# Graph network on one core: who adds the edge gates, how often TensorE signals, and how long the ring of gathered rows is

## The reference

```python
ea = silu(edge_attr @ We + be)                  # one row of 128 per edge: the "gates"
for l in range(4):                              # block 1: the four "layers"
    msg = relu(x[src] + ea)
    agg = segment_sum(msg, dst, num_segments=n)
    h = silu((x + agg) @ W1[l] + b1[l]) @ W2[l] + b2[l]
    x = layernorm(x + h) * gamma[l] + beta[l]
# blocks 2 and 3: three "convs" (two with degree norms, one plain with a self weight)
out = segment_sum(h[src], col, num_segments=n)
```

## Time and profile before

| | |
|---|---|
| median of three executions | 10520.3 us (10517.32 to 10532.23) |
| the profiled execution | 10607.1 us, of which the span from first to last instruction is 10605.0 us |
| busy in the span | PE 54%, PEld 37%, DVE 29%, ACT 9%, POOL 59% |
| TensorE clock granted | 0.716 of full speed on average |

### The profile page before, as it was taken

One profiled execution on the slowest core, in us unless ns is written; L12 is line 12 of the kernel. 1 busy time (PEld: TensorE's weight loads), 2 busy tenths in 40 slices (PEclk: granted clock), 3 DMA queues, 4 the chain that ended last, 5 costly groups with the idle time before them and its releaser, 6 DMA issues.

```text
span 10605.0 us, 107124 instructions
## 1 busy us (share of the span) xinstructions
PE 5675.4 (54%) x23750; PEld 3922.0 (37%) x23751; DVE 3028.2 (29%) x7366; ACT 949.0 (9%) x1767; POOL 6216.3 (59%) x6738
## 2 busy tenths in 40 slices
PE   3566637566775667656675666653334333333334
PEld 2333437333443334433343333333333333333234
DVE  3444577212221122312222122331122112231222
ACT  1111100111111111101111111110000000000000
POOL 3655536565555655466554655546666666656665
PEclk7566659777887788878788778875566556665666
DMA  5777755332323323233332323221111111111111
GB/s 167 218 219 218 203 139 155 90 88 82 85 75 86 87 82 85 79 85 87 83 83 75 88 81 81 77 59 45 47 49 48 46 46 49 48 46 46 47 49 47
DMA packets 796948, 945.08 MB, mean 89 GB/s; under 512 B 269045, under 2 KB 530448, under 8 KB 796302
## 3 DMA queue, kind: packets, MB, share of 16 engines
q0 software_dynamic: 213408, 463.35, 16.4%
q1 hardware_dynamic: 474970, 390.60, 13.2%
q10 hardware_dynamic: 108436, 89.99, 2.6%
HBM read 797.55 MB, written 152.25 MB: 90 GB/s over the span
## 4 chain that ended last, share of the span: by engine, by line
another core or an unknown queue 44%; PE 18%; issue 13%; DVE 9%; DVEq 3%; POOL 0%; SPq 0%; ACT 0%; DMA 0%; ACTq 0%; POOLq 0%
PE ps_big L1119 8%; PE ps_seg L1126 5%; DVE onehots L1715 2%; DVE sums L1746 2%; DVEq L453 1%; PE ps_seg L1197 1%; PE ps_big L1197 1%; PE ps_big L1063 1%; PE ps_t L1038 1%; DVE gate L1894 1%; DVE h_res L1898 0%; DVE group_stats L1783 0%; PE ps_seg L1063 0%; PE ps_big L987 0%
## 5 line engine op out<-in xcount | busy, mean ns | idle before, releaser
L871 POOL DMA_INDIRECT rows<-node_rows,idx_all x5488 | 5209.8, 949 | 3470.5 <-SPq L713 1590.0
L1119 PE MATMUL ps_big<-rows,ident 128*128 (+1 forms) x1960 | 1221.8, 709 | 1386.0 <-DVE onehots L1715 1249.5
L1746 DVE TENSOR_TENSOR sums<-sums,ps_seg 128x128 f32 x1342 | 385.5, 287 | 5141.3 <-remote 3368.8
L1126 PEld LDWEIGHTS ps_seg<-onehots 128*128 128x128 f32 x7840 | 1206.0, 223 | 899.0 <-issue 735.5
L1126 PE MATMUL ps_seg<-onehots 128*128 128x128 f32 x7840 | 1236.4, 309 | 260.6 <-issue 168.0
L1715 DVE SCALAR_TENSOR_TENSOR onehots<-ps_mm,away 128x512 f32<-128x512 f32 x1975 | 1349.3, 684 | 21.4 <-issue 13.8
L1197 PE MATMUL ps_seg<-rows,onehots 128*128 (+1 forms) x2952 | 613.8, 372 | 1235.4 <-DVE onehots L1715 595.8
L1119 PE MATMUL ps_big<-q_res,ident 128*128 (+1 forms) x1960 | 1153.9, 674 | 150.9 <-issue 123.0
L1119 PEld LDWEIGHTS ps_big<-rows,ident 128*128 128x128 f32 x1960 | 412.0, 224 | 2036.2 <-DVE onehots L1715 1461.7
L871 POOL DMA_INDIRECT sums<-kv_rows,idx_all x784 | 743.4, 948 | 548.2 <-SPq L711 281.2
L1197 PEld LDWEIGHTS ps_seg<-rows,onehots 128*128 128x128 f32 x2952 | 536.7, 272 | 1301.7 <-DVE onehots L1715 619.0
(11 more groups left out here) (215 smaller groups left out, 2974.4 us busy)
## 6 DMA issues: line engine op xcount, KB each, us to landing
q_res<-gates_by_edge SPq DMA_DIRECT2D x784, 256.0 KB
rows<-node_rows,idx_all POOLq DMA_INDIRECT x5488
rows<-dst_padded SPq DMA_DIRECT2D x196, 256.0 KB
value_rows_by_edge<-sums SPq DMA_DIRECT2D x196, 256.0 KB
gates_by_edge<-gate ACTq DMA_DIRECT2D x196, 256.0 KB
rows<-value_rows_by_edge SPq DMA_DIRECT2D x196, 256.0 KB, 3.5
node_rows<-h_res ACTq DMA_DIRECT2D x49, 448.0 KB
sums<-kv_rows,idx_all POOLq DMA_INDIRECT x784
```

The source lines that it names most:

```text
L871: pool.indirect_dma_start(target[:, r, j, :], None, table, bass.IndirectOffsetOnAxis(ap=idx_all[:, c * J + j:c * J + j + 1], axis=0), elem ...
L1119: last = nc.tensor.matmul(ps_big[u][:, :], ident[:, :], chunk_words(source, slot, 0, CHUNK), start=n == 0, stop=n == 1)
L1126: last = nc.tensor.matmul(ps_seg[u][:, 0:D], onehots[:, u, j, :], msg[:, u, j, 0:D], start=j == 0, stop=j == J - 1)
L1746: V.tensor_tensor(mine, mine, seg_four[(n - 1) % depth][:, 0:D], ALU.add).then_inc(agg_added, 1)
```

## The change

In the layers the gates are no longer added by TensorE. ScalarE copies a step's gates from SBUF to a PSUM bank, VectorE adds the rows to it into one of eight message buffers, ScalarE takes the relu in place, and TensorE does the product alone. In layers and convs TensorE raises `segsum_ready` once per four steps, at the end of a turn; four products lie side by side in one PSUM bank, and two banks take turns. VectorE waits once per turn, adds four products, and makes the four 0/1 matrices for the turn two ahead (eight sets instead of two or four). Slots of the ring are freed in the layers by VectorE's `rows_added`; in the convs by `segsum_ready` of the turn, and the ring of the convs has 14 slots instead of 7. The parts of a group stand one turn later in the code. The words that steer the turns are laid out anew by 25 small DMAs (14 ahead of the layers, 11 ahead of the convs).

```diff
-                def relu(u, added):
-                    act.wait_ge(gates_added, added)
-                    nc.scalar.activation(msg[:, u, :, 0:D], ps_big[u][:, :].rearrange("p (j d) -> p j d", d=D), ACT.Relu)\
-                        .then_inc(msg_ready, 1)
+                def copy_gates(slot, landed):
+                    act.wait_ge(rows_ready, landed)
+                    nc.scalar.copy(ps_gates[:, :], q_flat[:, ds(slot, CHUNK)]).then_inc(gates_copied, 1)
+
+                def relu(n, half, added):
+                    act.wait_ge(rows_added, added)
+                    nc.scalar.activation(msgs[:, half, n, :], msgs[:, half, n, :], ACT.Relu).then_inc(msg_ready, 1)
...
+                def add_rows(i, slots, half):
+                    for n in range(UNROLL):
+                        dve.wait_ge(gates_copied, dve.compute_val(i * UNROLL + add_base + (n + 1)))
+                        V.tensor_tensor(msgs[:, half, n, :], ps_gates[:, :],
+                                        rows[:, ds(up_to(slots[n], (RING - 1) * SLOT), CHUNK)], ALU.add).then_inc(rows_added, 1)
+
+                def add_sums(i, windows, half, ahead=True):
+                    upto = [dve.compute_val(i * UNROLL + base + (n + 1)) for n in range(UNROLL)]
+                    dve.wait_ge(segsum_ready, dve.compute_val(i + turn_base + 1))
+                    for n in range(UNROLL):
+                        mine = sums[:, ds(up_to(windows[n], (WINDOWS - 1) * AGGW), D)]
+                        dve.wait_ge(agg_added, upto[n])
+                        V.tensor_tensor(mine, mine, ps_seg[half][:, n * D:n * D + D], ALU.add).then_inc(agg_added, 1)
+                    for n in range(UNROLL if ahead else 0):
+                        mark_step(i * (UNROLL * J) + (n + 2 * UNROLL) * J, n, (onehots, marks_late)[half])
+
+                def steps_of(i, words, half, more=True):
+                    add_rows(i, words[0:UNROLL], half)
+                    if len(words) > UNROLL:
+                        add_sums(i - 1, words[UNROLL:2 * UNROLL], 1 - half, more)
...
+                    for j in range(J):
+                        last = nc.tensor.matmul(ps_seg[half][:, n * D:n * D + D], marks[:, n, j, :],
+                                                msgs[:, half, n, j * D:j * D + D], start=j == 0, stop=j == J - 1)
+                    if n == UNROLL - 1:
+                        last.then_inc(segsum_ready, 1)
...
-                chunk_pass(k, "edges", gates_added, l * N_STEP, also=lambda: layer_loads(l))
+                chunk_pass(k, "edges", rows_added, l * LAST, also=lambda: layer_loads(l))
...
+                for r in range(WIDE):
+                    sp.sem_inc(slot_free, 1)
+
+                def free_turn(turn):
+                    freed, regs = load_free(turn * RING - WIDE, RING)
+                    for r in range(RING):
+                        sp.wait_ge(segsum_ready, ((freed[r] + (UNROLL - 1)) >> (UNROLL.bit_length() - 1)) + begun)\
+                            .then_inc(slot_free, 1)
```

424 lines of the change are left out of this document (292 added, 132 removed).

## The result

The changed kernel takes 10898.7 us (median of four, 10876.3 to 10912.4) where the kernel before takes 10518.8: a ratio of 1.0365, 95% interval 1.0347 to 1.0383. It is **slower by 380 us**; 260 us less were forecast. The profiled execution is the shortest of the four, 10876.3 us, with a span of 10874.5.

The account below looks back on a forecast made before the run. POOL's gathers (980 us a pass) were the floor, with slot waits added by a loop of held TensorE signals. Layers -110 and convs -150 gave -260 us, 10520 to 10260; range 9,700 to 10,560.

Parts of the forecast that it names:

- The signal is held by time: Layers and convs: matmul signals are held while POOL gathers, from some 5 us after restart, until POOL pauses.
- Convs, -150 us: Convs: three turns a round cut slot waits from 155 to 90 us; -50 a pass, three times.
- Bounds: 0: Convs: the bound with no gain, two turns and 32 us a round, as before the change.
- Layers, a step's work: Layers: copy 0.585, addition 0.685, relu 0.597 us in strict sequence, 2.2 us a step with handovers, hidden behind POOL.
- Layers, 2.7 turns a round and 9.5 us of pause: Layers: slot waits of 215 us make a pass 1254 us against 1285.4; -28 us, four times, -110.
- The bound of 1359: Layers: the slow bound of a pass in us, at two turns a round and pauses of 10.5 us.
- Code: Rival, 0.04: VectorE's longer layer loop stops 4.56 us for instruction fetch in 30 rounds; 550 us over four layers, 10,800.
- VectorE's wait costs more than the loop did: Rival, 0.17: two turns a round and 11 us pauses in layers, +90 us a layer, -50 a conv; 10,730.
- The pass' end: Layers: 57 us between passes, 47.3 and 10 more for slower last steps and a last signal covering four.
- The 25 small DMAs: Ahead of layers and convs: issued while SP waits for the last store, costing nothing; uncovered, 25 x 0.4 = 10 us.
- Rare signals aren't held: Rival, 0.20: one signal per turn goes free; layers 1060, convs 1030 us a pass; whole 9,230, halfway 9,900.
- Slots are late for another reason: Rival, 0.05: if SyncE itself is slow, slot waits stay and only ends of passes move; 10,520.

Follow-up runs that it names:

- after_again: The changed kernel, unchanged, run again for its trace on one chip with the kernel before, where signals are late: 10908.5 us, ratio 1.0381.
- short_loop: The changed kernel with the last layer's residual code taken out of VectorE's loop for the first three layers (body 227 instructions, not 355): 10882.7 us, ratio 1.0357.
- pad_before: The kernel before with 200 never-reached small instructions added in VectorE's loop over a layer's turns: 10803.4 us, ratio 1.0282.
- two_banks_again: The changed kernel with ScalarE copying gates to two PSUM banks in turn, one step ahead of its relu, on a late-signal chip: 11131.7 us, ratio 1.0573.

## Why the prediction was wrong, step by step

**The signal is held by time (wrong; this is the step that failed).** I wrote that a matmul's signal is held while POOL gathers, "from some 5 us after its restart, and is let go when POOL pauses". The lateness was read rightly, its law was not. A signal also came out in the middle of a run, in the earlier trace rows already. What the runs support is that the instructions ahead of the signal count: with half of them a layer takes 51 to 75 us less, with twice as many, and twice the work, the kernel 1,135 us more, and four times the signals cost nothing that shows. The error in the convs follows from it, and in the layers it left me without the right question, which was what else stands in line.

**Convs, -150 us (measured +15 to +46).** I took three turns a round, 61/3 x 4.44 = 90 us of slot waits. A round is two turns and a little more, 128 to 143 instructions in the median; the pauses are 5.0 us: 61/2 x 5.0 = 152, measured 147.8, where it was 155.4. The ring of 14 and VectorE's greater lead were spent on a place that was not the limit. "Bounds: 0" was the case that came, and the pass' end added 6.5 and 19.6 us in the gaps, where I had allowed 15.

**Layers, a step's work (right).** ScalarE's copy takes 0.582 us, VectorE's addition 0.691, the relu 0.629; a step 1.98 us where I had 2.2 (groups of instructions by form of the changed kernel, as in the earlier trace rows):

```profile
L1896 DVE TENSOR_TENSOR score<-ps_big,stock 128x512 f32<-128x512 f32 x976 | 674.8, 691 | 2200.6 <-issue 1395.8 <-ACT ps_big L1524 804.7
...
L1528 ACT ACTIVATE score<-score 128x512 f32<-128x512 f32 x976 | 614.3, 629 | 3225.7 <-DVE score L1896 2647.8 <-issue 577.9
...
L1524 ACT COPY ps_big<-stock 128x512 f32 x976 | 568.0, 582 | 629.9 <-issue 590.6 <-POOLq L952 39.3
```

**Layers, 2.7 turns a round and 9.5 us of pause (the second step that failed: a term was missing).** In the second layer 23 pauses exceed 6 us, 61/23 = 2.65 turns each. That it fits so well is luck: the line of 6 us was drawn afterwards, and in after_again it gives 20 pauses, 3.05 turns. They last 10.6 us on average, 245 us where I had 215; the missing 1.1 us is less than the 4.9 of the branch, which falls into every other one. And there are 27 shorter ones, 82 us together, for which the sum had no term: a slot is freed by an addition, an addition every 2 us comes after each late signal, and POOL waits for the next piece each time. Pass: 982 + 327 + 58.5, less what counts twice = 1353.8, for 1254 forecast. Of the 100 us that are missing 30 are the pause's price and some 70 the short ones. The bound of 1359 holds it, but by another sum. What else moved in the layers: TensorE's granted clock in the second one fell from 0.80 to 0.61 in the mean, and a product that runs in one piece takes 1.16 to 2.08 us where most took 1.05. Its share no run separates.

**Code (given 0.04; its trigger and stop came, its price did not).** The loop's body grew and each round stopped at the branch, with the packets to show it, 4.88 us for 4.56. But not 550 us: by short_loop's layers 45 to 55, an estimate, of the 253 to 299 us that the layers lost. I had given it 0.04 because the earlier trace rows show hardly any fetch now; but the kernel before has a body of 163 instructions, and its row says nothing of one of 355. The counterpart, pad_before, which stops in each of 61 turns, cost 2.8% on its own.

**VectorE's wait costs more than the loop did (given 0.17).** Its +90 a layer is near to what came (+63 to +75), and VectorE's work behind the late signal is what lies in the pauses. Of all the cases it comes nearest. But its two turns a round hold in two_banks_again, and here there were 2.65 to 3.05.

**The pass' end (right in the layers).** 58.5 us, forecast 57. **The 25 small DMAs (right):** SyncE issues the 14 ahead of the layers from 1892.46 to 1901.92 and the 11 ahead of the convs from 7330.86 to 7338.79, 0.7 us each for the 0.4 that I took, and then still waits until 1923.09 and 7365.06 for the last store. The gap ahead of the first conv grew by 21.5 us (76.65 for 55.13) all the same, ahead of the first of ScalarE's last two stores. **Rare signals aren't held (given 0.20):** ruled out where signals are late. **Slots are late for another reason (given 0.05):** the sum of the slot waits stayed as it said (1590 and 1615 us), but in the layers they grew, and by that case the number of TensorE's instructions shouldn't have moved them; SyncE's own share no run tests.

## What to carry to other kernels

When one engine's signals come late, ask what stands ahead of them before cutting their number: vary instructions and signals apart from each other (the same work split in two, the same instructions with four times the signals), since either alone is a small edit, and look whether the split has also grown the engine's own work. Before unrolling a loop on an engine with large conditional parts, count the instructions of its body; never-executed code was worth 2.8% here. Then ask how much of a stop lies in waits that are there anyway, before you count on its price. A faster chain can be slower: two_banks_again has 1.0573 where after_again has 1.0381, with POOL's pauses rarer, longer and bare.

## What the hardware showed that I had not expected

**The pile.** While POOL issues indirect gathers, TensorE's signals reach VectorE 12 to 26 us late, and TensorE goes from some point on at one instruction in 0.70 or 1.40 us with its inputs there, on three of the five chips to which the experiments went; a conv's round ends after 128 to 152 of its instructions. On the two others hardly any of this is seen, and the kernel before takes 8,710 instead of 10,510 us, 17% less. What the two kinds differ in no run here tells. A candidate, argued and not shown: every execution timed here was profiled. The Trainium skill (NOTIFIC — the notification-queue block, "3. Interfaces" and "10. Constraints, capacities, measured rates") says that a core's engines write their trace records through a block which can stall an engine when an internal queue is full, and which holds about 500 records. By that, an estimate, three to four records for each of the 128 to 152 instructions would fill it. The same page says that a record costs the engine nothing; if the records are behind it, the steps of 1.40 us disagree. Without an execution that isn't profiled it stays open, and with it whether the late signals and the loss of 3.7% are there at all outside the profiler.

**Stops at a branch.** With a loop body of about 350 instructions VectorE stopped at the branch, mostly for 4.6 to 5.8 us, and a group's normalisation in it ran in pieces with gaps of up to 1.8 us (the changed kernel at 4336 to 4339), where the kernel before has none over 0.24 in the one at 4298; with 227 the packets fell from 164 to 22 a layer and the stop at the branch was gone. Where in between it sets in was not tried.
